# Both chunks of a counted pair in one product of 128 columns, in a graph kernel on one core

## What is computed

```python
msg = node_feat[src] + edge_feat
agg = jax.ops.segment_sum(msg, dst, num_segments=node_feat.shape[0])
h = jax.nn.relu(agg @ W1 + b1)
x = _layernorm(x + h @ W2 + b2, axis=-1)
```

## Time and profile before

| | |
|---|---|
| median of 3 runs | 2372.08 us |
| lowest, highest | 2364.94, 2373.15 us |
| the profiled execution's own time | 2373.34 us |
| its span, first to last instruction | 2371.5 us |
| mean granted TensorE clock in it | 0.738 |

### The profile page before, as it was taken

The page is one execution under the profiler, slowest core; times in us unless marked ns, Lnnn a source line. Parts: engine busy times, 40 slices in busy tenths (PEclk is TensorE's granted clock), DMA queues, the critical chain, the costliest instruction groups (busy, mean ns, idle before and its releaser), DMA issues.

```text
span 2371.5 us, 45768 instructions
## 1 busy us (share of the span) xinstructions
PE 1501.9 (63%) x18752; PEld 1318.1 (56%) x18753; DVE 1234.8 (52%) x2701; ACT 738.2 (31%) x935; POOL 968.9 (41%) x1045
## 2 busy tenths in 40 slices
PE   2555656566657576666566676555756666657776
PEld 1555545455646566656555665455655565546664
DVE  4765545555546355645545554434545554445535
ACT  5322111122223233323222343323433333323323
POOL 7644454443443433443433434343244334243432
PEclk6556776776777767777767777777878777778798
DMA  7322222222212222222222222221222222212232
GB/s 188 75 78 78 76 71 71 61 71 63 79 50 76 68 65 66 69 67 69 69 55 61 73 61 64 54 57 50 69 62 53 61 61 63 59 50 63 69 64 55
DMA packets 150052, 161.03 MB, mean 68 GB/s; under 512 B 42291, under 2 KB 134035, under 8 KB 149507
## 3 DMA queue, kind: packets, MB, share of 16 engines
q1 hardware_dynamic: 118229, 123.61, 18.0%
q0 software_dynamic: 31616, 34.50, 7.5%
HBM read 153.06 MB, written 4.93 MB: 67 GB/s over the span
## 4 chain that ended last, share of the span: by engine, by line
PE 48%; another core or an unknown queue 21%; issue 16%; ACT 8%; DVE 4%; POOL 1%; DMA 1%; DVEq 0%; POOLq 0%; SPq 0%; ACTq 0%
PE sums_ps L1155 18%; PE counted_ps L1138 16%; PE chunk_ps L1120 13%; ACT counts L721 7%; DVE oh_key L937 1%; DVE oh_lo L933 1%; POOL xmsg L610 1%; PE turn_ps L1166 1%; POOL x_parts L659 0%; PE turn_ps L1091 0%; DVE counts L946 0%; DMA lists<-in_src 0%; DMA records<-edge_records,run_at 0%; DVE lists L902 0%
## 5 line engine op out<-in xcount | busy, mean ns | idle before, releaser
L610 POOL DMA_INDIRECT xmsg<-in_x,idx_t x925 | 889.4, 961 | 922.8 <-PE chunk_ps L1120 634.6
L721 ACT CAST counts<-counted_ps 128x784 bf16<-128x784 f32 (+2 forms) x728 | 615.5, 864 | 1385.8 <-remote 667.0
L1138 PE MATMUL counted_ps<-oh_key,oh_lo 128*128 128x98 bf16 (+1 forms) x5264 | 677.8, 257 | 582.1 <-ACT counts L721 335.1
L933 DVE TENSOR_TENSOR oh_lo<-chunk_ps,tables 128x768 bf16<-128x768 f16 (+3 forms) x622 | 446.2, 717 | 764.5 <-remote 359.9
L1138 PEld LDWEIGHTS counted_ps<-oh_key,oh_lo 128*128 128x128 bf16 x5264 | 437.7, 115 | 683.7 <-issue 351.0
L1155 PE MATMUL sums_ps<-x_parts,counts 128*128 128x193 bf16 (+3 forms) x4900 | 749.3, 284 | 56.6 <-issue 55.8
L1155 PEld LDWEIGHTS sums_ps<-x_parts,counts 128*128 128x128 bf16 (+3 forms) x4900 | 542.4, 136 | 74.5 <-issue 64.5
L937 DVE TENSOR_TENSOR oh_key<-chunk_ps,tables 128x1176 bf16<-128x1176 f16 (+2 forms) x622 | 459.9, 739 | 0.0
L1120 PE MATMUL chunk_ps<-onehot,cmsg 128*64 128x16 f32 (+4 forms) x4400 | 227.2, 241 | 116.1 <-issue 115.5
L1120 PEld LDWEIGHTS chunk_ps<-onehot,cmsg 128*64 128x64 f32 x4400 | 206.4, 173 | 146.7 <-issue 141.0
L619 POOL DMA_INDIRECT records<-edge_records,run_at x42 | 39.6, 944 | 394.4 <-DVE run_at L827 371.3
(11 more groups left out here) (111 smaller groups left out, 446.4 us busy)
## 6 DMA issues: line engine op xcount, KB each, us to landing
cmsg<-in_edge_attr SPq DMA_DIRECT2D x440, 160.0 KB
gmsg<-in_edge_attr SPq DMA_DIRECT2D x185, 160.0 KB
xmsg<-in_x,idx_t POOLq DMA_INDIRECT x925
out_nodes<-x_parts SPq DMA_DIRECT2D x11, 256.0 KB, 2.6
edge_records<-counts SPq DMA_DIRECT2D x1, 1500.0 KB
lists<-in_src SPq DMA_DIRECT2D x1, 1400.0 KB
lists<-in_dst SPq DMA_DIRECT2D x1, 1400.0 KB
records<-edge_records,run_at POOLq DMA_INDIRECT x42
```

What stands on the lines that cost most here:

```text
L610: pool.indirect_dma_start(xmsg[:, at * D:(at + 1) * D], None, x, bass.IndirectOffsetOnAxis(ap=idx_t[:, of:of + 1], axis=0)).then_inc(gathe ...
L721: nc.scalar.copy(to.rearrange("p h (m n) -> p h m n", m=m), ps.rearrange("p m (n h) -> p h m n", h=HI)).then_inc(unit_kept, 1)
L933: nc.vector.tensor_tensor(oh_lo[s % RING][:, 0:n * P].rearrange("p (k n o) -> p k n o", k=n, o=2), lo_ps.rearrange("p (n o) -> p n o", o=2 ...
L1138: mm = nc.tensor.matmul(unit_ps[u][:, col:col + slot.key_cols], oh_lo[s % RING][:, n * P:(n + 1) * P], oh_key[s % RING][:, n * slot.key_co ...
```

## The change

For counted pairs whose width is at most 32, `twin` is true. Their two chunks are loaded interleaved by tile: for tile j, the 64 features of the first chunk and then those of the second, so that a tile's 128 columns lie side by side. A load then writes five pieces of 256 bytes per partition instead of one of 1,280. `products` takes for each tile one product: 128 columns of edge rows against both chunks' one-hots (2w columns). Of its result, 128 x 2w, the two blocks on the diagonal are the sums; the second chunk's lies in partitions 64 to 127, columns w to 2w, and `add` reads it there. The other two blocks are not used. Pairs of width 40 and the gathered pairs stay as they were.

```diff
--- before.py
+++ after.py
@@ -179,6 +179,9 @@
         c = (i | 1) + (CCH if kind == "gather" else 0)
         return next((w for w, rows in NARROW_ROWS.items() if c < rows * TILES), WIN)
 
+
+    def twin(kind, i):
+        return kind == "count" and 2 * width_of(kind, i) <= WIN
 
     HI = -(-N // P)
     LOG_P = P.bit_length() - 1
@@ -484,7 +487,11 @@
 
             def load_counted(i):
                 s = i % CSLOTS
-                sp.dma_start(cmsg[:, s * TILES * D:(s + 1) * TILES * D], edge_v[i]).then_inc(cin[s], 16)
+                if twin("count", i):
+                    two = cmsg[:, s // 2 * 2 * TILES * D:(s // 2 + 1) * 2 * TILES * D].rearrange("p (j h f) -> p j h f", j=TILES, h=2)
+                    sp.dma_start(two[:, :, i % 2, :], edge_v[i].rearrange("p (j f) -> p j f", j=TILES)).then_inc(cin[s], 16)
+                else:
+                    sp.dma_start(cmsg[:, s * TILES * D:(s + 1) * TILES * D], edge_v[i]).then_inc(cin[s], 16)
 
             def load_most(g):
                 a, b = RANGES[g]
@@ -898,8 +905,8 @@
                 if before and (place % LAG >= 2 or before in BLOCK_ADDS):
                     dve.wait_ge(added, before)
                 w = width_of(kind, i)
-                to = halves[place % 2][:, bass.ds(at, w)]
-                nc.vector.tensor_tensor(to, to, pair_ps[place // 2 % 2][place % 2 * D:(place % 2 + 1) * D, 0:w],
+                to, own = halves[place % 2][:, bass.ds(at, w)], (place % 2 * w if twin(kind, i) else 0)
+                nc.vector.tensor_tensor(to, to, pair_ps[place // 2 % 2][place % 2 * D:(place % 2 + 1) * D, own:own + w],
                                         ALU.add).then_inc(added, 1)
 
             def add_parts(b):
@@ -1112,6 +1119,16 @@
                     pe.wait_ge(added, ADDED["chunk", first - 1])
                 pe.wait_ge(marked, first // 2 + 1)
                 rows = [rows_of(*job) for job in pair]
+                if twin(*pair[0][1:]):
+                    (place, kind, i), w = pair[0], width_of(*pair[0][1:])
+                    assert len(pair) == 2 and i % 2 == 0
+                    edges = cmsg[:, i % CSLOTS * TILES * D:(i % CSLOTS + 2) * TILES * D]
+                    marks = onehot[place // 2 % OSLOTS][:, 0:2 * TILES * w].rearrange("p (h j n) -> p h j n", h=2, j=TILES)
+                    for j in range(TILES):
+                        mm = nc.tensor.matmul(pair_ps[place // 2 % 2][:, 0:2 * w], edges[:, 2 * j * D:2 * (j + 1) * D], marks[:, :, j, :],
+                                              start=(j == 0), stop=(j == TILES - 1))
+                    mm.then_inc(summed, 2)
+                    return
                 steps = [[(of, j) for of in parts for j in range(TILES)] for parts in rows]
                 for n in range(max(len(x) for x in steps)):
                     for half, (place, kind, i) in enumerate(pair):
```

## The result

The changed kernel takes 2426.2 us (median of 4 runs, 2416.3 to 2429.3) against 2372.2 for the kernel before in the same comparison: a ratio of 1.0234, 95% interval 1.0213 to 1.0255, so 54 us slower. The forecast was 2394, 22 us slower. Side and range held; the size was off by 32 us. The profiled execution took 2429.3 us, with a span of 2427.5 and a mean granted clock of 0.738, as before the change.

What follows compares the result with a forecast made beforehand. The prediction took gather runs to bound the kernel: completions come late, TensorE gets a ration of instructions per run and does the rest between runs. Sum: 2373.3 + 80 - 54 - 5 = 2394 us, range 2335 to 2465.

Steps and rivals of the forecast that it cites:

- bursts of the 120 or so pairs between runs: 122 narrow counted pairs starting between gather runs: merged products take 0.51 or 1.06 us longer per pair, +80 us in all.
- bursts of the others: 68 narrow counted pairs in or heading a gather run: longer bursts cost nothing, since TensorE stands still there anyway.
- fewer instructions, with the mode gap: 68 pairs free 1,360 instruction places in gather runs, at 40 ns each -54 us; -5 more for array gaps lost.
- mode gap: A 0.16 us gap before half-width loads on TensorE, lost between two twins in a row: -5 us.
- loads: 380 counted-row loads in 256-byte pieces: cost 0, hidden because six slots let them be issued some 30 us early.
- ration: Per gather run TensorE gets through about 60 to 130 instructions, however long the run; the rest falls between runs.
- Rival D: Loads in 256-byte pieces make gathers or loads late: +40 us, 2434 us; chance 0.05.
- Rival A: Instructions are scarce everywhere, so all 190 pairs save 20 x 40 ns, -152 us: 2311 to 2350 us; chance 0.22.
- backlog: Work delayed behind each gather run, through which half as many instructions would go in half the time.
- rule on loads: TensorE weight loads priced at 107 ns for 128 columns whatever the clock: twin 1.10 us at low clock, sum 2346.
- Rival B: Longer bursts between runs are hidden as ScalarE and VectorE run ahead; half of +80 returns: 2354 to 2374; chance 0.17.
- Rival C: What is scarce in gather runs is completions or time, not instructions, so nothing comes back: 2468 us; chance 0.16.

## Why the prediction was right in its side and wrong in its size

| term | on record | measured, one after the other |
|---|---|---|
| bursts of the 120 or so pairs between runs | +80 | +72 |
| bursts of the others | 0 | +21 |
| fewer instructions, with the mode gap | -59 | -45 |
| loads | 0 | +7 (alone +21) |
| sum | +21 | +55 |

The measured column adds up by construction, and its first three rows rest on a burst that was five sixths as long as the twin's: by the estimate above up to 19 us more for the bursts, and as much more for the fewer instructions. No run measures the mode gap (-5) alone.

- **What bounds the kernel.** Right, and more so than I said: the gather runs hold the whole core, and without them 2,370 us become 1,372.
- **The burst.** 1.10 and 2.13 us were forecast from the tail's rows and are what the trace shows. The 80 us for the pairs between runs, between bounds of 62 and 95, came out as about 72.
- **The step that failed first: "In a run TensorE's own time is free, since it stands still anyway."** The run with long bursts for the 32 pairs in runs cost 11 us, the one for the 38 behind gathered products 10. In the timeline TensorE's stop of 6.3 us ends at 1643.06, once ScalarE's copy, released late at 1642.10, is done, and I read the cost so: a burst in front of a product that somebody waits for makes that completion later still. No run tests this reading.
- **The step that failed second: "68 pairs use 20 instructions less of a run's ration, so 1,360 others move".** What failed is the 1,360. It takes the 68 pairs to have all their 2,720 matmuls and loads in runs. Counted in the trace before, all 190 pairs had 1,716 of 7,600 there, and the 38 behind a gathered pair only 510 of 1,520. So about 700 moved, half as many: the runs hold 655 more matmuls and loads of other kinds than counted products after the change (12,314 against 11,659), 793 more with plain loads, 71 more with long bursts only, 696 more with the first chunk only. That the total in the runs stays was right within the spread of the profiles: 13,475 before, 13,626 after, 13,509 with the first chunk only, and 13,183 to 13,984 in the kernels that leave no instruction out. The price of 40 ns for each that moved holds in one run and not in the other: 27/696 = 39 ns beside short bursts, and 45/720 = 62 ns or more beside long ones. But the gain doesn't arise where the ration would have it: the 32 pairs had 1,014 of the 1,716 and gave 5 us (0 to 9) of the 27 (21 to 34). How leaving out instructions between runs gains time, only beside gathers, stays open.
- **The step that failed third: the loads, "Cost 0, hidden by that lead".** No one waits for them, and beside the gathers they still cost 21 us alone and some 7 beside twins; how, no run shows. Rival D named 40 us for them and a chance of 0.05, by gathers or loads that come late: no load is waited for, and no run shows a gather late for this reason. The Trainium skill, page "DMA: Bandwidth & Descriptors" (Specifications), which asks for at least 512 bytes in a piece, was weighed and set aside here. The pieces do have a price beside the gathers; that it is the rule's read-modify-write no run shows, and without gathers there is none.
- **Rival A**, instructions scarce everywhere, falls by its size: half the instructions in all 190 pairs gave 27 us, 0.14 us a pair, where it needed 0.43 to decide and had 0.80 (with the estimate for long bursts, 64 us are 0.34). Its place doesn't fall: most of the 27 us came from pairs outside the runs, as it would have it. The runs without gathers say only that there is no such gain without them, and its backlog belongs to the gather runs too. The rule on loads beside it falls by the 2.13 us of a twin at the low clock, where it needs 1.10. **Rival B** falls: bursts between runs are paid at 0.58 us each. **Rival C**, 2468, is what long bursts without any gain take (2459 measured); the twins get 45 us of that back, 38 with their interleaved loads.
- **Two numbers of the rivals** don't follow from their own terms. Rival A breaks even at (80 - 5)/190 = 0.39 or (95 - 5)/190 = 0.47 us a pair, so 0.43 is a middle; rival B's "half of the +80" gives 2354, and nothing gives its 2374.

By the table the failed steps make +21, +14 and +7, and the bursts between runs -8: 34 together, where the forecast was off by 32. The 45 us gained back are close to the 54 on record partly by luck, since fewer instructions moved at a higher price each.

## What to carry to other kernels

A stretch in which an engine seems to stand still isn't free time for more work on it: here it cost half of what it cost elsewhere, and only a run with the work put there alone could tell. Merging two products that sit in different halves of the array into one of full width halves the instructions and gives up the overlap of the halves; here 0.59 us became 1.10, and half the instructions bought back about half of the microseconds that this cost. A DMA that nobody waits for can still cost; the waits can't show that, a run with the loads alone can.

## What the runs showed of the hardware

- The 925 indirect DMAs of GpSimd, busy for 889 us, cost this core 1,000 us (2,370 against 1,371.6), though nothing but their own products needs their data. While they are issued completions come late: SyncE was released at 1640.70 by products that had ended at 1634.66. Of all that was tried here nothing else moved the time by a tenth as much.
- In float32, 20 loads of 64 columns with their matmuls, in turn in the two halves of the array, take as long (0.78 us) as 10 in one half (0.77) at the full clock. Issued half after half they take 1.10. The Trainium skill, page "TensorEngine Tiling (Array Packing)" (Key Properties), says that different tiles can load and multiply in parallel; the trace agrees, and adds that the order of issue decides how much of it comes about.
- 380 loads in pieces of 256 bytes instead of 1,280 cost 21 us (15 to 28) beside indirect DMAs and 2 us without them, which can't be told from nothing.
